# Cross-attention and FFN block: the addition for the second pair of heads moved between the two clips of even tiles

## The reference

```python
q = proj(layernorm(x), Wq, bq); k = proj(ctx, Wk, bk); v = proj(ctx, Wv, bv)
scores = clip(einsum('bhsd,bhtd->bhst', q, k) / sqrt(32), -50, 50)
scores = clip(where(attend, scores, -10000), -50, 50)
probs = softmax(scores, axis=-1)
ctx = einsum('bhst,bhtd->bhsd', probs / (probs.sum(-1) + 1e-8), v)
```

## Time and profile before

| | |
|---|---|
| median of 3 runs | 1802.44 (1800.71 to 1803.1) |
| the profiled execution: its time, its span | 1800.76, 1799.0 |
| PE busy, share of the span | 1535.3, 85% |
| DVE busy | 969.3, 54% |
| ACT busy | 746.2, 41% |
| exponentials (L536), 416 | 444.0 busy, 1114 ns each |
| clips (L581), 416 | 280.0 busy, 689 ns each |
| additions (L572), 192 | 234.1 busy, 1219 ns each |
| scores, matmuls (L620), 2496 | 207.3 busy |
| values, matmuls (L633), 1664 | 225.5 busy |

### The profile page before, as it was taken

One profiled execution on the slowest core, in us unless ns is written; L12 is line 12 of the kernel. 1 busy time (PEld: TensorE's weight loads), 2 busy tenths in 40 slices (PEclk: granted clock), 3 DMA queues, 4 the chain that ended last, 5 costly groups with the idle time before them and its releaser, 6 DMA issues. The chain is left out here.

```text
span 1799.0 us, 25569 instructions
## 1 busy us (share of the span) xinstructions
PE 1535.3 (85%) x10712; PEld 1025.1 (57%) x10712; DVE 969.3 (54%) x1377; ACT 746.2 (41%) x917; POOL 189.8 (11%) x135
## 2 busy tenths in 40 slices
PE   4879888888889898888988815756999999999998
PEld 3668433575334763337733303433788888888887
DVE  6522688525886248872288817997333333332433
ACT  2322678525786348763387702223211121221211
POOL 0032000320001300004000023452000000000000
PEclk9999899998999989999999966887999999999999
DMA  6351000320002200013000042673700110110001
GB/s 189 133 169 52 1 8 13 110 53 13 7 13 89 62 24 7 8 40 117 1 7 8 7 155 74 216 289 122 304 24 23 47 44 4 47 47 0 24 24 71
DMA packets 55828, 119.13 MB, mean 66 GB/s; under 512 B 14280, under 2 KB 35144, under 8 KB 49832
## 3 DMA queue, kind: packets, MB, share of 16 engines
q1 hardware_dynamic: 52936, 108.01, 17.0%
q0 software_dynamic: 2784, 9.57, 2.3%
HBM read 78.51 MB, written 39.06 MB: 65 GB/s over the span
## 5 line engine op out<-in xcount | busy, mean ns | idle before, releaser
L536 ACT ACTIVATE cx_probs<-cx_sc,proj_mbias 128x1024 f32<-128x1024 f32 (+1 forms) x416 | 444.0, 1114 | 113.7 <-DVE cx_padd L572 59.0
L581 DVE TENSOR_SCALAR cx_probs<-cx_probs 128x1024 f32<-128x1024 f32 (+1 forms) x416 | 280.0, 689 | 92.2 <-ACT cx_probs L536 91.2
L620 PE MATMUL cx_sc<-cx_q,cx_kt 32*128 32x512 f32 (+1 forms) x2496 | 207.3, 434 | 77.9 <-ACT cx_probs L536 74.8
L572 DVE TENSOR_TENSOR cx_padd<-cx_probs 128x1024 f32<-128x1024 f32 x192 | 234.1, 1219 | 1.9 <-PE cx_tot L645 0.8
L633 PE MATMUL cx_acc<-cx_probs,cx_vt 128*32 128x512 f32 (+1 forms) x1664 | 225.5, 615 | 5.3 <-DVE cx_probs L581 5.3
L620 PEld LDWEIGHTS cx_sc<-cx_q,cx_kt 32*128 32x128 f32 (+1 forms) x2496 | 104.1, 185 | 210.6 <-ACT cx_probs L536 196.6
L1188 DVE SCALAR_TENSOR_TENSOR ff_hf<-ff_up,ff_scale,ff_silu 128x512 f32<-128x512 f32 x64 | 48.1, 751 | 289.4 <-ACT ff_silu L1153 289.4
L126 PE MATMUL cx_sc<-proj_cs,proj_wk 128*128 128x256 f32 (+1 forms) x1344 | 170.7, 285 | 33.4 <-DVE cx_kt L563 24.9
L1153 ACT ACTIVATE ff_silu<-ff_gp,ff_scale 128x512 f32<-128x512 f32 x64 | 44.1, 689 | 368.5 <-PE ff_gp L126 368.5
L126 PE MATMUL ff_yp<-ff_wds,ff_hs 128*128 128x512 f32 x768 | 189.6, 396 | 0.2 <-DVE ff_hs L1191 0.2
L126 PEld LDWEIGHTS cx_sc<-proj_cs,proj_wk 128*128 128x128 f32 x1344 | 165.8, 193 | 40.8 <-DVE cx_kt L563 28.8
(11 more groups left out here) (137 smaller groups left out, 1703.9 us busy)
## 6 DMA issues: line engine op xcount, KB each, us to landing
proj_raw<-in_ctxT SPq DMA_DIRECT2D x24, 512.0 KB, 3.6
scr_q<-qu_qs SPq DMA_DIRECT2D x4, 2048.0 KB, 6.3
cx_q<-scr_q SPq DMA_DIRECT2D x4, 2048.0 KB, 9.0
scr_wd<-pr_wds SPq DMA_DIRECT2D x4, 2048.0 KB, 13.2
ff_wds<-scr_wd SPq DMA_DIRECT2D x8, 1024.0 KB, 4.5
scr_xs<-hand_xs SPq DMA_DIRECT2D x3, 2048.0 KB, 7.8
ff_xs<-scr_xs SPq DMA_DIRECT2D x3, 2048.0 KB, 17.5
qu_xt<-in_x SPq DMA_DIRECT2D x4, 1024.0 KB, 11.0
```

Of the source, the lines that this page charges most:

```text
L536: nc.scalar.activation(probs[N % NB][0:r], sc[N % NSC][0:r], ACT.Exp, bias=mbias[0:r, b, t:t + 1], scale=SCALE).then_inc(exp_done, 1)
L572: nc.vector.tensor_tensor(padd[z][(g * QP + j) % 2][:], probs[(2 * i + z) % NB][:], probs[(2 * i + 2 + z) % NB][:], ALU.add).then_inc(adde ...
L581: nc.vector.tensor_scalar(probs[N % NB][0:r], probs[N % NB][0:r], LOW, HIGH, ALU.max, ALU.min).then_inc(clip_done, 1)
L620: last = nc.tensor.matmul(sc[N % NSC][0:r, h % 2], kt[own, z, c, t * P:t * P + r], q[own, y, c], start=n == 0, stop=n == 2)
```

## The change

In even tiles from 2 on, the addition for pair 1 (`add(b, c, t // 2 - 1, 1)`) is issued after the clip of pair 0 instead of after the clip of pair 1. It adds the probabilities of the two tiles before, t-2 and t-1. Nothing else is edited.

```diff
--- before.py
+++ after.py
@@ -581,7 +581,7 @@
                         nc.vector.tensor_scalar(probs[N % NB][0:r], probs[N % NB][0:r], LOW, HIGH, ALU.max, ALU.min).then_inc(clip_done, 1)
                         if t % 2 and n % 2:
                             add(b, c, t // 2, 0)
-                        if t and t % 2 == 0 and n % 2:
+                        if t and t % 2 == 0 and n % 2 == 0:
                             add(b, c, t // 2 - 1, 1)
 
                 for b in range(B):
```

## The result

| | before | with the change |
|---|---|---|
| median of 20 runs each | 1802.12 | 1810.16 (1803.55 to 1822.32) |
| profiled span | 1799.0 | 1808.2 |
| attention, first scores to last values, batches 1 to 4 | 146.83, 143.87, 143.58, 142.60 | 144.94, 142.04, 144.42, 141.20 |
| from there to the next batch's first scores | 88.43, 88.56, 88.77 | 92.43, 91.37, 95.09 |
| from the last batch's last values to the end | 765.95 | 766.51 |

The ratio is 1.0052, 95% interval 1.0035 to 1.0068: **slower by 0.5%**, where 0.3% faster was forecast. Attention became 4.3 us shorter, and the three stages behind it, in which no instruction was touched, 13.1 us longer.

What follows compares the result with a forecast made beforehand. No engine is full: a loop of waits between DVE and ACT sets the pace, a second through PE's sums close behind. Savings of 1.38 us per batch, 5.5 over four, off the 1802.44 median gave 1796.9 us, range 1790.5 to 1802.5.

Steps and rivals of the forecast that it cites:

- The regular cycle: Two tiles, even and odd, in the attention loop: 5.25 us forecast against 5.43 before, 0.18 saved.
- the held addition: DVE's first-pair addition, waiting for PE's sums behind the even tile's values: free at 3.51 us, not 3.09, setting the cycle.
- Group: A whole group of 13 tiles, second and third of a batch: 34.94 us instead of 35.58, 0.64 saved.
- End of a batch: Last group, from the last first-pair addition to tile 12's values: 3.61 us instead of 2.48, 1.13 lost.
- The sum in attention: Savings and loss over a batch's groups and end: 1.19 + 2 x 0.64 + 0.04 - 1.13 = 1.38 us saved.
- What follows the loop is unchanged work and only moves earlier: The stages after the attention loop: claimed to do the same work, only starting earlier.
- The term of 1.13 per batch for the end: Last values of each batch, behind the moved clip: claimed to start later, 1.13 us lost per batch.
- The rival "slower": Regular cycle above 5.46 us because the wait on the moved clip costs more; run over 1806 us; chance 0.09.
- The rule on busy time: Whole kernel: PE, busiest at 31.04 of 35.58 us, sets the pace, so the run stays at 1802.4; chance 0.04.
- DVE's wait for sums: Regular cycle: idle time of some 0.34 us on DVE before the first-pair addition, ended by PE's sums.
- ACT's wait: Regular cycle: ACT's idle time before an exponential, ended by DVE's addition, down from 1.13 to about 0.95 us.
- The held A0: DVE's addition of the first pair, held by PE's sums until 3.51 us after the second-pair addition's start.

Runs made afterwards that it cites:

- e4: The change, with the half sum of a tile put ahead of its values in PE's queue (tiles 3 to 11): 1768.03 us, ratio 0.9814.
- e5: The kernel before, additions as before, with the sums ahead of the values in PE's queue: 1802.38 us, ratio 0.9999.
- e2: The kernel before with the edit in the last tile of each batch alone (4 of 96 additions): 1818.40 us, ratio 1.0092.
- e3: The change, with 8 matmuls of unused result on PE before the wait for each batch's last values: 1795.22 us, ratio 0.9966.
- e10: Control: the kernel before with 3 filling matmuls at each batch's end: 1801.90 us, ratio 0.9996.
- e9: e8 with 3 more filling matmuls ahead of the scores of tile 2 in groups 2 to 4: 1757.48 us, ratio 0.9759.
- e1: The change, but in the last tile of each batch the addition is back behind both clips: 1804.05 us, ratio 1.0002.
- e7: e1 with POOL's start at a batch's end gated on the last clip instead of the last exponential: 1795.85 us, ratio 0.9952.
- e6: e4 with the 8 filling matmuls of e3 at each batch's end: 1761.77 us, ratio 0.9775.
- e8: e4 with e1's condition, e7's gate on POOL and 4 filling matmuls before each batch's last values: 1754.86 us, ratio 0.9743.

## Why the prediction was wrong

- **The regular cycle**: right, 5.25 forecast, 5.26 measured; the held addition decides, through the values that wait for the moved clip. e4 with e5 shows that this is the cause and no chance agreement.
- **Group**: right, 34.94. **End of a batch** up to its last values: right, 3.62 for 3.61.
- **The sum in attention**: 1.38 per batch forecast. The batches with the same falls of the clock before and after gave 1.83 (second) and 1.40 (fourth). The first gave 1.89, with 3 us less at half clock after than before. The third lost 0.85 because at two of its group boundaries the clock fell for some 3 us, which cost 1.6 each. Before, this happened once in the 12 boundaries, after three times.
- **"What follows the loop is unchanged work and only moves earlier"**: this step failed. The term of 1.13 per batch for the end was a delay, and I had priced it as one; but it was made of idle time on PE, and with it went the clock of the stage behind. Measured by e2, the end costs about 4 us per batch, not 1.13; by e3, with the idle time filled, the total would have come to 1795.2, inside the range and 1.7 from the 1796.9.
- I had read the clock in one group in the middle, where it was 1.00, and concluded that it plays no part. The rows that would have warned were in reach: the 0.84 of idle time in the earlier trace rows, which a further 1.13 and an earlier PE were bound to make 2.4, and falls of the clock already there in the first tiles of each batch (before, 6.8 us at half clock from 427.87 on in the second).
- The rival "slower" had 0.09 and the wrong place: it looked for the loss in the cycle. The rule on busy time would have forecast no change; busy time of DVE and ACT stayed (971.5 and 746.8), that of PE rose by 23 us, since its matmuls were slower.
- **What the trace should show**: DVE's wait for sums was 0.33, forecast 0.34. ACT's wait was 0.62 and not 0.95. The held A0 (525.68) also holds the exponential of the same tile's first pair (it starts 1.34 later, at 527.02), which I had not followed up; it costs nothing in the cycle as PE's next scores have to wait for the values anyway.

**Open**: the last 12 us before a batch's scores had 3.4 us at half clock in all three stages before and 6.7 with the change, some 5 of the 13.1 us. It is not tied to the batch's end: e3 had 6.7, 6.7 and 3.4 there, e5 0, 3.4 and 10.3, e10 6.7, 3.4 and 3.4. No run was made to explain it. Such falls move a single profile's stages by as much as the falls at the ends do: in e10, with a clock of 1.00 behind all inner ends, the first stage took 92.12. So the cause rests on the medians of e2, e3 and e10 together with the clock right behind the ends, and not on the length of one stage.

Nor is the length of the idle time in front all that decides. At each group's boundary PE sat idle 0.86 us before the scores of tile 2 in every kernel but e9, and behind it the clock fell in 19 of the 132 boundaries of their profiles: in 4 of 48 in the four kernels with the additions of the loop as before (before, e2, e5, e10), in 12 of 48 in those with the change and PE's order as before (the change, e1, e3, e7), in 3 of 36 with the sums first (e4, e6, e8). What makes this difference isn't shown.

## What to carry to other kernels

A loop of waits can be summed from start-to-start distances to a hundredth, so do this for every loop that closes through the moved instruction, and look for the second one: two edits that give nothing or a loss alone can give 1.9% together. Then ask of each delay on the matmul engine whether it is idle time, and what runs right behind it: idle time that grew by 1.13 us, from 0.84 to 1.97, cost about 4 us per batch here (e2), and filling such idle time with matmuls whose result nobody reads kept the clock up behind the inner ends and took back 15 us (e3).

## What was not expected of the hardware

- Behind the last values of a batch TensorE's granted clock fell to its lower level in none of 3 profiled ends with 0.84 us of idle time in front, 1 of 6 with 1.26 or 1.27 (e7, e5), 2 of 3 with 1.92, 2 of 3 with 2.07, 3 of 3 with 1.97 and with 2.40. These are few ends, and 0.84 is no safe length: behind 0.86 us at the groups' boundaries it fell 19 times in 132. The same program thus gets another clock at one end than at the next, which fits the spread of its runs (1803.55 to 1822.32).
- A clip of 0.68 us on DVE was held up by 0.65 while POOL issued a load (1.36), and not when the issue came later. The page SBUF — State Buffer of the Trainium skill, section Who interferes with whom, says that DVE's two-port modes and GpSimd exclude each other on a shared port pair, whoever is first; e1 and e7 agree with that, though the clip's mode is not in the trace. Who comes first is not told by these rows to a few hundredths, however: in the kernel before, the load's row starts 0.06 ahead of the second clip's (568.73 and 568.79), and there the clip took its 0.68 and the load 1.51.
